# Adding layer 1's identity with GpSimd instead of with TensorE products, in a two-layer graph network on one core

## The reference

```python
# layer 0: D^-1/2 A D^-1/2 (x W + b), d = row sums of A, then layernorm(x + .)
# layer 1:
adj_hat = adj + jnp.eye(adj.shape[0], dtype=adj.dtype)
d_inv_sqrt = 1.0 / jnp.sqrt(jnp.sum(adj_hat, axis=1))
adj_norm = adj_hat * d_inv_sqrt[:, None] * d_inv_sqrt[None, :]
out = adj_norm @ (X @ W) + b          # relu, then layernorm(x + .)
```

## Time and profile before

| | us |
|---|---|
| runs | 1811.89, 1814.25, 1814.79 (median 1814.25) |
| profiled execution, its own time | 1815.33 |
| its span in the profile | 1813.5 |
| TensorE busy | 1640.0 (90%) |
| VectorE busy | 1206.5 (67%) |
| ScalarE busy | 754.2 (42%) |
| GpSimd busy | 167.5 (9%) |

### The profile page before, as it was taken

How to read it: one execution, slowest core, us unless ns; L and a number is a source line. 1 busy time by engine, 2 the same in 40 slices (tenths; PEclk the granted TensorE clock), 3 DMA queues, 4 the chain that set the end, 5 groups by cost and what they waited for, 6 DMA issues and landing times.

```text
span 1813.5 us, 16886 instructions
## 1 busy us (share of the span) xinstructions
PE 1640.0 (90%) x6136; PEld 1116.5 (62%) x6136; DVE 1206.5 (67%) x1550; ACT 754.2 (42%) x904; POOL 167.5 (9%) x177
## 2 busy tenths in 40 slices
PE   0247789999999999977999999999999999999996
PEld 0123344444444444436788888888888878888885
DVE  1444556767767854636776666466465999999996
ACT  5554332220000000014554545444444777777774
POOL 0000000000000000012110000000000011111111
PEclk9778899999999999988999999999999999999998
DMA  9999999998987769326777665666565999999991
GB/s 384 421 421 421 421 421 401 389 399 357 403 362 310 277 244 383 122 102 220 267 257 271 260 234 208 239 248 232 208 235 225 422 419 420 398 388 387 395 397 77
DMA packets 85906, 573.38 MB, mean 316 GB/s; under 512 B 10400, under 2 KB 10656, under 8 KB 20288
## 3 DMA queue, kind: packets, MB, share of 16 engines
q1 hardware_dynamic: 76320, 541.23, 74.9%
q0 software_dynamic: 9504, 31.07, 4.7%
HBM read 556.79 MB, written 15.47 MB: 316 GB/s over the span
## 4 chain that ended last, share of the span: by engine, by line
PE 77%; DMA 11%; DVE 8%; issue 2%; ACT 1%; POOL 1%; SPq 1%; ACTq 0%; DVEq 0%
PE acc L677 29%; PE acc L701 15%; PE acc L703 15%; PE acc L702 15%; DMA lent<-adj_tiles 7%; DVE low L820 3%; DMA own<-adj_tiles 2%; DMA own<-adj_far 1%; DMA lent<-adj_far 1%; DVE run L831 1%; PE turned L613 1%; ACT high L720 1%; DVE stats L798 1%; PE mixed L644 1%; PE acc L691 1%
## 5 line engine op out<-in xcount | busy, mean ns | idle before, releaser
L701 PE MATMUL acc<-high,feat_high 128*128 128x512 f32 x1336 | 529.8, 397 | 17.6 <-DVE feat_low L912 9.4
L677 PE MATMUL acc<-lent,feat 128*128 128x512 f32 x1168 | 525.5, 610 | 20.3 <-DVE feat L868 14.5
L703 PE MATMUL acc<-high,feat_low 128*128 128x512 f32 x1336 | 523.1, 392 | 0.0
L702 PE MATMUL acc<-low,feat_high 128*128 128x512 f32 x1336 | 522.6, 391 | 0.0
L820 DVE TENSOR_TENSOR low<-own,high 128x1024 fp32r<-128x1024 f32 x330 | 390.4, 1220 | 152.2 <-ACT high L720 150.8
L720 ACT CAST high<-own 128x1024 fp32r<-128x1024 f32 x330 | 338.3, 1054 | 212.8 <-PE acc L703 198.0
L677 PEld LDWEIGHTS acc<-lent,feat 128*128 128x128 f32 x1168 | 227.3, 196 | 305.6 <-issue 289.2
L831 DVE TENSOR_TENSOR run<-run,lent 128x2048 f32<-128x2048 f32 x135 | 309.4, 2292 | 133.9 <-DMA lent<-adj_tiles 128.4
L701 PEld LDWEIGHTS acc<-high,feat_high 128*128 128x128 f32 x1336 | 252.4, 189 | 71.7 <-issue 11.2
L703 PEld LDWEIGHTS acc<-high,feat_low 128*128 128x128 f32 x1336 | 252.2, 189 | 54.0
L702 PEld LDWEIGHTS acc<-low,feat_high 128*128 128x128 f32 x1336 | 252.7, 189 | 50.6
(11 more groups left out here) (69 smaller groups left out, 674.4 us busy)
## 6 DMA issues: line engine op xcount, KB each, us to landing
lent<-adj_tiles SPq DMA_DIRECT2D x237, 1024.0 KB, 11.9
own<-adj_tiles SPq DMA_DIRECT2D x197, 1024.0 KB, 6.7
lent<-adj_far SPq DMA_DIRECT2D x60, 1024.0 KB, 23.0
own<-adj_far SPq DMA_DIRECT2D x18, 1024.0 KB, 23.7
x_in<-x_rows POOLq DMA_DIRECT2D x32, 256.0 KB, 6.4
sums_rows<-stage POOLq DMA_DIRECT2D x27, 256.0 KB, 6.3
sums_in<-sums_rows POOLq DMA_DIRECT2D x27, 256.0 KB, 8.9
x_t<-x_cols SPq DMA_DIRECT2D x16, 256.0 KB, 15.6
```

The costliest lines, as they stand in the source:

```text
L677: mm = nc.tensor.matmul(bank, feat0[:, j * Q + q, :], raw(n)[:, q * T:(q + 1) * T], start=(u == plan.first[g] and q == 0), stop=(u == plan ...
L701: nc.tensor.matmul(bank, f_high, a_high[:, chunk], start=(u == plan.first[g] and q == 0), stop=False)
L702: nc.tensor.matmul(bank, f_high, a_low[:, chunk], start=False, stop=False)
L703: mm = nc.tensor.matmul(bank, f_low, a_high[:, chunk], start=False, stop=(u == plan.last[g] and q == Q - 1))
```

## The change

GpSimd gets a new item `add_eye` for each row of sweep 3. It waits until the row's diagonal tile has landed, and adds 1 to the diagonal elements by one tensor_tensor over the four 128 x 128 blocks that hold the diagonal (512 columns), in place in the raw tile. Its key is the row's first take less 4 (`EYE_EARLY`). ScalarE's `high` of a diagonal tile waits for it. The 8 products of L691 are gone. In place of `ident_r` there is `diagonal`, four copies of the identity side by side, made at the start by GpSimd.

```diff
+EYE_EARLY = 4
@@ class Plan
             dve.append((lo_key(k + 1, 5), "make_shift", i))
             act.append((hi_key(k + 2, 5), "make_out", i))
+            before = self.first[("left1", i)] - EYE_EARLY
+            pool.append(((before, 4.5, 0), "add_eye", i))
             pool.append(((k + 2, 5, 0), "store_out", i))
@@ buffers
-        ident_r = put("ident_r", [P, P], F32R)
+        diagonal = put("diagonal", [P, Q, P])
+        def on_diagonal(tile):
+            blocks = tile.rearrange("p (q c f) -> p q c f", q=Q, c=Q).rearrange("p q c f -> p (q c) f")
+            return blocks[:, 0:Q * Q:Q + 1, :]
+        eye_added = sem("eye_added")
@@ GpSimd
-            nc.gpsimd.tensor_copy(ident_r[:, :], ident[:, :]).then_inc(ident_ready, 1)
+            for q in range(Q):
+                ins = nc.gpsimd.tensor_copy(diagonal[:, q, :], ident[:, :])
+            ins.then_inc(ident_ready, 1)
+                elif kind == "add_eye":
+                    n = takes[plan.first[("left1", i)]][0]
+                    if third[i] == 0:
+                        pool.wait_ge(ident_ready, 2)
+                    pool.wait_ge(tile_landed[plan.slot[n]], 16 * plan.landings[n])
+                    blocks = on_diagonal(raw(n))
+                    nc.gpsimd.tensor_tensor(blocks, blocks, diagonal[:, :, :], ALU.add).then_inc(eye_added, 1)
@@ TensorE
-                    if half == 1 and u == plan.last.get(("left1", i)):
-                        bank = acc[plan.bank[("left1", i)]]
-                        for q in range(Q):
-                            for f in (feat_high[1], feat_low[1]):
-                                nc.tensor.matmul(bank[:, q * P:(q + 1) * P], f[:, i * Q + q, :], ident_r[:, :],
-                                                 start=False, stop=False,
-                                                 skip_group_check=True)
@@ ScalarE, in "high"
                     act.wait_ge(tile_landed[plan.slot[n]], 16 * plan.landings[n])
+                    if takes[i][1] == takes[i][2]:
+                        act.wait_ge(eye_added, third[takes[i][1]] + 1)
```

## The result

The changed kernel takes 1816.23 us (median of 20 runs, 1814.09 to 1820.10), the kernel before beside it 1813.57 (20 runs, 1810.75 to 1815.37): a ratio of 1.0018, 95% interval 1.0011 to 1.0024. It is 2.7 us slower. The forecast was 1818.5 us, 4.3 us slower.

What follows compares the result with a forecast made beforehand. TensorE and VectorE were taken as near-bounds, VectorE the bound after the change. +0.7 us at the start, +5.2 in six stretches and -1.6 in the tail gave +4.3: 1818.5 us, range 1806 to 1822.5.

Steps and rivals of the forecast that it cites:

- What bounds the kernel: Long stretches of sweep 3: TensorE needs 46.39 us, VectorE 45.85; without the products TensorE needs 44.53, so VectorE is late next.
- What the removed products are worth: Sweep 3: 0.93 us a row, 14.9 in all; without new cost only 4.8 less in six stretches, 1.6 in the tail.
- The add holds VectorE up by 1.1 us: At each GpSimd add in sweep 3, the next `low` waits 1.1 us for the add's reading; bounds 0 and 1.5.
- The sum over the six stretches: Six long stretches from 1492.66 us on: 45.85 us plus 1.1 for each add, together 5.2 us slower.
- The start of sweep 3: Up to 1492.66 us: adds of rows 0 and 14 delay row 0's `y_t` to about 1449.7; net 0.7 us slower.
- the held `low`: Sign in the profile: at each add a `low` of 2.2 us or a gap of 1.1 before it.
- the lengths of the last stretches: Sign in the profile: stretches near 48.0 us, the last two forecast at 48.05 each.
- the `y_t` of long rows without a wait: Sign in the profile: at long rows' `y_t` VectorE no longer waits for TensorE.
- TensorE's stops for `low`: Sign in the profile: TensorE waits for `low` in all six stretches, 2 us and more together in each.
- No hold-up at all: Rival for sweep 3: the add doesn't hold VectorE up; 6.8 us faster, 1807.4 us; chance 0.22.
- All 14.9 us won: Rival for sweep 3: TensorE is the only bound, so the products' whole time is won; 1799.4 us; chance 0.05.
- Late adds: Rival: adds late behind GpSimd's queue stop ScalarE in each row, about 1 us a row; 1830 or more; chance 0.03.

Runs made afterwards that it cites:

- no_identity: The changed kernel with layer 1's identity left out altogether, neither GpSimd's add nor the products: 1806.9 us, ratio to before 0.9961.
- write_only: The changed kernel with each add replaced by three GpSimd zero-writes that read no SBUF, ScalarE still waiting, identity left out: 1809.1 us, ratio 0.9974.
- short_low: The changed kernel without add or products, each `low` of sweep 3 made for 960 of 1024 columns: 1802.1 us, ratio 0.9943.
- both folded kernels: Kernel before, products replaced by features x scale + bias made in sweep 2: 1805.4 us; the same with rows 15 and 0 keeping products: 1806.4 us.
- add_aside: The changed kernel with the add made from constants into a spare buffer, ScalarE not waiting, identity left out: 1811.3 us, ratio 0.9986.
- two_adds: The changed kernel with the add made twice in a row for each tile: 1831.7 us, ratio 1.0101.
- second profile: The changed kernel run again unaltered for another profile: 1817.4 us in one run.

## Why the prediction was right, step by step

*What bounds the kernel.* Right. VectorE's need was read as 45.85 us; without the identity the last stretches are 45.74 and 45.69, and with shorter `low` they fall to TensorE's 44.75 and 44.49 (44.53 forecast).

*What the removed products are worth.* Right: the stretches of no_identity are within 0.15 us of those written down, the tail is 21.68 there and 21.62 in the changed kernel (23.21 - 1.6), and `y_t` of row 0 comes 50.91 us behind `var`, 0.47 less than before.

*The add holds VectorE up by 1.1 us.* Right, and shown: a held `low` takes 2.32 instead of 1.22; three writes with 1.69 us in all hold nothing; a shorter add holds 0.85; doubled adds cost 0.86 us more for each in the last stretches. The add was estimated at 1.2 and takes 1.29 to 1.40. What is shown is the difference between an add with two SBUF inputs and a write with none; a GpSimd instruction with one SBUF input was not run. The Trainium skill (SBUF — State Buffer, Who interferes with whom) says that a GpSimd instruction that reads SBUF and a VectorE instruction with two SBUF inputs block each other, and one that only writes blocks nothing. These runs agree with both halves (1.10 us, and 1229 ns at most beside the writes). Why an add gets in behind one `low` at 1570.20 and behind six at 1525.79 stays open.

*The sum over the six stretches* was forecast too large: +5.2 forecast, +1.8 in the first profile (283.79 against 282.02 us from the `y_t` of row 14 to that of row 8), +4.0 in the second (285.98), which has the late add. Two terms were mis-sized. The hold-ups come to 10.6 us in the first profile, not 12.1: two adds (1583.60 and 1632.65) waited until VectorE was at `y_t`, which has one SBUF input, and ran beside it, so the next `low` took only 1.49. And VectorE's need is not 45.85 everywhere: stretch less hold-ups is 45.35, 45.2, 45.66, 45.67, 45.68, 45.67. It is 0.2 us lower in the last four. In the first two, where the short row ends soon, it is half a us lower or more: one of VectorE's two stalls of 0.40 for ScalarE is missing there, and the prediction used one value for all.

*The start of sweep 3* was forecast too small: +0.7 forecast, +2.6 measured (98.63 against 96.00). The delay of `y_t` was right in size: that of row 0 came 1.93 later (1.7 forecast), and TensorE's stop ended 1.9 later. Some of this is luck, since two terms missed opposite ways: the cast of row 0's tile came 44.15 us behind the last `var` instead of 41.67, so 2.5 later and not 1.2, because its add met a running `low` (2.05 us). Against that, some 1 us of waiting that VectorE had before was used up (0.57 of it between the two `y_t`), which the prediction had put at nothing. What the prediction left out is the clock. TensorE's row behind the stop, and its granted clock in the changed kernel:

```profile
1462.25 0.47 PE L712 MATMUL acc<-high,feat_high 128*128 128x512 f32 x1 [2.19 <-DVE low L833]
...
1464.39 0.63 PE L713 MATMUL acc<-low,feat_high 128*128 128x512 f32 x1
1464.81 0.63 PE L714 MATMUL acc<-high,feat_low 128*128 128x512 f32 x1
1465.24 0.63 PE L712 MATMUL acc<-high,feat_high 128*128 128x512 f32 x1
```
```profile
1462.00:1464.00 2.00, 1.75 (x7) 1.42 (x8) 2.00 (x4) 0.66 (x2) 1.00 (x1) 0.85 1.04 434
1464.00:1466.00 2.00, 2.00 (x6) 1.62 (x5) 1.62 (x3) 2.00 (x5) 0.71 (x2) 0.50 0.99 414
1466.00:1468.00 2.00, 2.00 (x8) 1.60 (x8) 2.00 (x2) 2.00 (x3) 0.97 (x2) 0.80 1.02 426
```

Half the clock, 1.2 GHz, is granted for some 3.5 us, and some eight products follow each other at 0.43 instead of 0.227 us: 8 x 0.2 = 1.6 us. 1.9 + 1.6 - 0.93 = 2.6. The same fall stands in no_identity, write_only, short_low and both folded kernels, and takes 1.6 of what the missing products should have given there. It came behind a series of stops (0.69, 1.48, 1.85 and 2.58 us from product to product); before there is one of 2.07 and no fall. But add_aside and two_adds have stops of 2.56 behind others of 0.8 to 1.9 and kept the full clock. The seven profiles with a fall have a last stop of 2.3 to 2.6 us. Of the five without, three have at most 2.07 and these two 2.56, so what decides is not settled.

Start, stretches and tail make 2.6 + 1.8 - 1.6 = 2.8 us in the first profile; the medians differ by 2.7. The forecast of 4.3 was the sum of two errors that partly cancel, 3.4 too much in the stretches and 1.9 too little at the start; that it came as near as 1.6 us is in part luck.

*The chances and the signs.* The prediction said that under 3.6 us can't be told from none. With 20 runs of each kernel 2.7 us is clear of none, but by that mark it counts as "same" (0.33), not as "slower" (0.37). The low end of the forecast's own range was added up wrongly: a hold-up of 0.9 gives about 1816.2, not 1815.5. Of the signs, the held `low`, the lengths of the last stretches and, in the six, the `y_t` of long rows without a wait came true. Less was seen of TensorE's stops for `low` (6.0 us in the six stretches, not 2 and more in each; 4.6 us more ahead of the transposes), and an add took up to 8.07 us, not 2.3.

*Rivals.* No hold-up at all (1807.4) is what a kernel without a reading GpSimd would do, as write_only (1809.1); for the add it is refuted. All 14.9 us won is refuted by no_identity. Late adds: in the first profile ScalarE waited once for GpSimd by name (2.5 us, the first tile of sweep 3) and 2.7 us at the second, never in the long stretches. In the second profile it did so once there, for 2.8 us, so this rival is a part of the cost in some executions; how often is not known.

## What to carry to other kernels

Before work is taken off the busiest engine, read at each place how long the next engine waits for it there: only that wait can be won, here 7 us of 14.9. Work handed to GpSimd is not free merely because GpSimd is idle: its add of 512 columns, which reads SBUF, held up VectorE's instructions with two SBUF inputs for 1.10 of its 1.3 to 1.4 us. If another engine waits for such work, leave time for it to be kept waiting too: here up to 13 us. A term that is only added to a result can be folded into an operand that is read anyway (the bias of `z`), made at a time when its engine waits; that version is 0.37% faster than the kernel before.

## What was not expected of the hardware

GpSimd's add can be kept waiting by back-to-back `low` for 8 and even 13 us, although a `low` that comes behind it is held only 1.1. A `shift` of 4 columns takes 1.25 us if it meets an add. A product of 128 columns costs TensorE 0.11 us in a block of its like and between products of 512 columns alike, half of a product of 512 columns with 0.227. And TensorE's clock fell to half behind stops of 2.3 to 2.6 us in seven of the nine profiles that have such stops at the start of sweep 3, which cost 1.6 us in the changed kernel.
